# Two transfers, 120 rows and 8 rows, for the store of every 17th tile of a cross network kernel

## What is computed

```python
B, D, L = (16384, 4096, 6)
def step(x, wb):
    wi, bi = wb
    xw = jnp.matmul(x, wi)          # (B, 1)
    x_new = x0 * xw + bi + x
    return (x_new, None)
x, _ = jax.lax.scan(step, inputs, (w, b))   # x0 = inputs
```

## Time and profile before

| | us |
|---|---|
| median of 3 runs | 1284.51 (1283.15 to 1284.72) |
| the profiled execution | 1283.12 |
| its span, first to last instruction | 1281.4 |
| PE / PEld busy | 769.9 (60%) / 722.1 (56%) |
| DVE busy | 1149.6 (90%) |
| ACT / POOL busy | 99.0 (8%) / 5.1 (0%) |
| DMA | 537.69 MB, mean 420 GB/s |
| L275, finish of a tile | 126 of 4.464 |
| L262, transpose of 2048 columns | 252 of 2.288 |

### The profile page before, as it was taken

One profiled execution on the slowest core, in us unless ns is written; L12 is line 12 of the kernel. 1 busy time (PEld: TensorE's weight loads), 2 busy tenths in 40 slices (PEclk: granted clock), 3 DMA queues, 4 the chain that ended last, 5 costly groups with the idle time before them and its releaser, 6 DMA issues.

```text
span 1281.4 us, 19275 instructions
## 1 busy us (share of the span) xinstructions
PE 769.9 (60%) x8724; PEld 722.1 (56%) x8724; DVE 1149.6 (90%) x532; ACT 99.0 (8%) x326; POOL 5.1 (0%) x16
## 2 busy tenths in 40 slices
PE   5676666656566666556546655665655765665563
PEld 2665665555555565546546554565555654665453
DVE  5899998899988988989889898898898988989887
ACT  2000000000000000000000000000000000000000
POOL 1000000000000000000000000000000000000000
PEclk9878787777867867787787787777787678678776
DMA  9999999999999999999999999999999999999996
GB/s 353 402 425 430 429 433 427 428 431 432 430 430 432 429 432 431 430 420 427 425 421 422 415 427 421 422 425 423 422 425 421 422 427 422 420 426 424 425 420 281
DMA packets 38156, 537.69 MB, mean 420 GB/s; under 512 B 4296, under 2 KB 4488, under 8 KB 5632
## 3 DMA queue, kind: packets, MB, share of 16 engines
q1 hardware_dynamic: 18656, 268.64, 50.3%
q10 hardware_dynamic: 19488, 268.94, 49.4%
HBM read 269.12 MB, written 268.44 MB: 420 GB/s over the span
## 4 chain that ended last, share of the span: by engine, by line
DMA 77%; DVE 11%; PE 9%; ACT 2%; issue 1%; ACTq 0%; DVEq 0%
DMA out_dram<-tiles 62%; DMA tiles<-in_r_inputs_dram 14%; PE dots L333 9%; DVE tiles L275 6%; DVE blocks L262 4%; ACT spread L185 1%; DMA tiles<-in_L_rec_w_dram 1%; DVE tiles L297 1%; ACT weights L171 0%; PE turned L347 0%; PE scratch L311 0%; ACT c_last L176 0%; ACTq L162 0%; ACTq L165 0%; DVE tiles L223 0%
## 5 line engine op out<-in xcount | busy, mean ns | idle before, releaser
L333 PE MATMUL dots<-blocks,weights 128*64 128x128 f32 x8192 | 691.5, 348 | 401.5 <-DVE blocks L262 400.2
L333 PEld LDWEIGHTS dots<-blocks,weights 128*64 128x64 f32 x8192 | 656.6, 184 | 426.7 <-DVE blocks L262 425.3
L262 DVE STREAM_TRANSPOSE blocks<-tiles 128x2048 f32<-128x2048 f32 x252 | 567.1, 2288 | 107.1 <-issue 106.6
L275 DVE SCALAR_TENSOR_TENSOR tiles<-tiles,scale,c_last 128x4096 f32<-128x4096 f32 x126 | 562.5, 4464 | 0.0
L185 ACT ACTIVATE spread<-dots,group_mask 128x128 f32<-128x128 f32 x256 | 73.2, 369 | 1069.5 <-PE dots L333 1069.5
L347 PE MATMUL turned<-layer_sel,spread 128*128 128x8 f32 x512 | 67.9, 259 | 79.7 <-ACT spread L185 79.7
L347 PEld LDWEIGHTS turned<-layer_sel,spread 128*128 128x128 f32 x512 | 62.0, 191 | 95.1 <-ACT spread L185 95.1
L192 ACT ACTIVATE growth<-turned,ones 128x16 f32<-128x16 f32 x64 | 17.5, 274 | 80.3 <-PE turned L347 57.5
L269 DVE TENSOR_TENSOR_SCAN scale<-growth,cw 128x6 f32<-128x6 f32 x128 | 13.0, 141 | 4.9 <-ACT growth L192 4.9
L311 PE MATMUL scratch<-tiles,ones 6*128 6x512 f32 x16 | 8.9, 1134 | 13.4 <-ACT c_last L176 7.3
L311 PEld LDWEIGHTS scratch<-tiles,ones 6*128 6x128 f32 x16 | 2.5, 306 | 18.2 <-ACT c_last L176 8.8
(11 more groups left out here) (20 smaller groups left out, 7.2 us busy)
## 6 DMA issues: line engine op xcount, KB each, us to landing
tiles<-in_r_inputs_dram SPq DMA_DIRECT2D x128, 2048.0 KB, 13.7
out_dram<-tiles ACTq DMA_DIRECT2D x126, 2048.0 KB, 26.7
out_dram<-tiles ACTq DMA_DIRECT2D x8, 512.0 KB, 4.9
tiles<-in_L_rec_w_dram ACTq DMA_DIRECT2D x4, 96.0 KB
tiles<-in_L_rec_b_dram ACTq DMA_DIRECT2D x4, 24.0 KB
strips_b<-in_L_rec_b_dram SPq DMA_DIRECT2D x1, 96.0 KB, 11.3
strips_w<-in_L_rec_w_dram SPq DMA_DIRECT2D x1, 96.0 KB, 12.3
```

The costliest lines, as they stand in the source:

```text
L262: nc.vector.transpose(blocks[:, c, :, :].rearrange("p t n -> p (t n)"), tiles[:, at:at + TB, c * CH:(c + 1) * CH]).then_inc(blocks_ready, 1)
L275: nc.vector.scalar_tensor_tensor(out=tiles[:, s, :], in0=tiles[:, s, :], scalar=scale[:, batch % 2, t, L - 1:L], in1=c_last[:], op0=ALU.mu ...
L333: last = nc.tensor.matmul(dots[at:at + KM * Q, :, :, :], weights[:, c * KB + k:c * KB + k + KM, :], blocks[:, c, :, k * Q:(k + KM) * Q], s ...
```

## The change

`in_two(n)` holds for n = 9, 26, 43, 60, 77, 94 and 111 of the 128 tiles. `store` issues two transfers for these on ACT: rows 0 to 119, then rows 120 to 127, each adding 16 to the slot's semaphore. `stored_by(n)` is what the semaphore of tile n's slot stands at when tile n and all before it in that slot have been stored; SP and the end of ACT's program wait for it, in place of 16 for each store. Tiles 126 and 127, in four pieces each, are as before.

```diff
--- before.py
+++ after.py
@@ -19,6 +19,8 @@
 HALF_BANKS = 4
 S = 16
 PIECES = 4
+PART = 120
+EVERY, FIRST = 17, 9
 
 
 def cross_network(nc, x, w, b, out):
@@ -119,6 +121,12 @@
             turned_rows = w_turned[rows, :].rearrange("p (k q) -> p k q", q=Q)
             return into, turned_rows[:, :, 0:L * G].rearrange("p k (l j) -> p j l k", j=G)
 
+        def in_two(n):
+            return n % EVERY == FIRST
+
+        def stored_by(n):
+            return sum(32 if in_two(m) else 16 for m in range(n % n_slots, n + 1, n_slots))
+
         @block.sync
         def _(sp):
             for s in range(n_slots):
@@ -131,7 +139,7 @@
                     sp.dma_start(strips_w[:], w_strips).then_inc(strips_w_landed, 16)
             for n in range(n_slots, n_tiles):
                 s = n % n_slots
-                sp.wait_ge(y_stored[s], n // n_slots * 16)
+                sp.wait_ge(y_stored[s], stored_by(n - n_slots))
                 sp.dma_start(tiles[:, s, :], x[n * P:(n + 1) * P, :]).then_inc(x_landed[s], 16)
 
         @block.gpsimd
@@ -194,7 +202,12 @@
 
             def store(n):
                 act.wait_ge(tiles_done, n + 1)
-                act.dma_start(out[n * P:(n + 1) * P, :], tiles[:, n % n_slots, :]).then_inc(y_stored[n % n_slots], 16)
+                s = n % n_slots
+                if in_two(n):
+                    act.dma_start(out[n * P:n * P + PART, :], tiles[0:PART, s, :]).then_inc(y_stored[s], 16)
+                    act.dma_start(out[n * P + PART:(n + 1) * P, :], tiles[PART:P, s, :]).then_inc(y_stored[s], 16)
+                else:
+                    act.dma_start(out[n * P:(n + 1) * P, :], tiles[:, s, :]).then_inc(y_stored[s], 16)
 
             spread_dots(0)
             make_growth(0)
@@ -212,7 +225,7 @@
                               tiles[:, s, at]).then_inc(y_stored[s], 16)
             for s in range(n_slots):
                 last_stores = 1 if s < n_slots - TB else PIECES
-                act.wait_ge(y_stored[s], 16 * (n_rounds - 1 + last_stores))
+                act.wait_ge(y_stored[s], stored_by(n_tiles - n_slots + s) + 16 * (last_stores - 1))
 
         @block.vector
         def _(dve):
```

## The result

| | median us | lowest to highest | runs |
|---|---|---|---|
| before | 1284.51 | 1283.15 to 1284.72 | 6 |
| after | 1305.58 | 1297.14 to 1311.55 | 6 |

The ratio is 1.0158, 95% interval 1.0136 to 1.0181. The kernel is 21 us slower where 4.3 were forecast: the sign is right, the size is not, and the time lies outside the range. Some runs of a kernel fall into a slower state and are left out of times and ratios; here that is one, of the four with 25 cuts. The profiled execution took 1297.14 us, the fastest of the six, in a span of 1295.4 us. So the trace holds 14 of the 21 us, and what it shows of a cut (a tile stored in two pieces) is the low side.

What follows compares the result with a forecast made beforehand. One slow DMA engine of sixteen was taken to bound the kernel. Its seven added rows, 7 x 0.620 = +4.3 us, with everything else hidden, on the 1284.5 us median gave 1288.8 us, range 1262 to 1292 us.

Steps and rivals of the forecast that it cites:

- What bounds the kernel: DMA transfers: one slow engine of sixteen sets the pace, 0.620 us a row against 0.608 for the others.
- How rows fall on engines: A transfer uses the largest count up to 16 dividing its rows: 120 rows on 15 engines, 8 on 8.
- Which engine is slow: DMA engines: the slow one lies in both the 8 and the 15, so it gets seven rows more; 0.52.
- The trail of packets: Single packets followed per engine: the slow one took rows of w, and most likely of b.
- The rival of the spared engine: The slow engine is the one the 120-row pieces leave out: 20.4 us less, 1264.1 us; chance 0.22.
- the one of unchanged rows: Rival: the slow engine is one whose rows stay the same: 1284.5 us, no change; chance 0.17.
- Issues, waits, closing packets: Seven more ACT issues, 2.4 us, hidden; SP's waits for 32 and small closing packets cost nothing visible.
- The split transfer's own rate: Stores of split tiles: 0.608 to 0.620 us a row as now; at worst 4.9 us a tile, 34 in all.
- The row term, 7 x 0.620: Seven added rows on the slow DMA engine, from the 8-row pieces: +4.3 us.
- The pace stops mattering once the last load is issued: End of the run: all seven split tiles lie in front of that load, so their added rows count.
- The 120-row pieces run badly: Rival at the seven split tiles: 7 x 4.9 = 34 us, 1319 us at worst, some 1300 at half; chance 0.09.

Runs made afterwards that it cites:

- the four with 25 cuts: Runs of the kernel that makes the change's cut at row 120 in every fifth tile, 25 tiles in place of 7: 1345.85 us, ratio 1.0505 to before.
- four late ones: The change's cut, 120 and 8 rows, at tiles 60, 75, 90 and 105 only, against the kernel before: 1294.63 us, ratio 1.0078.
- early cuts: The change's cut, 120 and 8 rows, at tiles 9, 13, 17 and 21 only, against the kernel before: 1303.13 us, ratio 1.0129.
- the eight small pieces: Against the kernel before, eight tiles stored as 112, k and 16 - k rows, k from 1 to 8, last two on own semaphores: 1298.36 us, one execution.

## Why the prediction was wrong, step by step

- **What bounds the kernel: right.** One engine sets the pace before and after (share 0.06 at the end), and all lost time is ahead of the last load, which starts 14.0 us later in the profiled run.
- **How rows fall on engines: right.** 49 more packets are 15 and 8 engines; small pieces start on the same first engines.
- **Which engine is slow: right.** The trail of packets had it in both pieces; it is the fifth. The rival of the spared engine, 0.22, is ruled out by that, and so is the one of unchanged rows, 0.17.
- **Issues, waits, closing packets: nearly right.** ACT's busy time is the same 99.0 us. But a second transfer on a saturated stream is not free: 0.9 us a cut in the cut by columns, of which 0.6 falls at the cuts.
- **"The split transfer's own rate": this step failed.** I took the lower end, nothing, "since the piece is nearest to the 128-row store". It is near in size and not in shape. Alone, eight 120-row stores take 1.32 times as long as whole ones, and a row of the 8-row piece 2.5 us. In the kernel a cut costs 3.0 us in place of 0.62, and 2.0 with no row moved (112 and 16 rows).
- **The row term, 7 x 0.620: too small.** Sparing the slow engine its part in the 8-row piece gives back 10 us by the medians, 1.5 a cut, and 1.0 a cut by the two profiled runs.
- **"The pace stops mattering once the last load is issued": right here, not in general.** The change's last load starts 14.0 us later and its span ends 14.0 us later. The cut by columns and the kernel with 120, 4 and 4 rows lose 3.7 and 9.8 us in the last tiles.

An estimate from the shapes alone: on the slow engine 8 rows x 0.62 x 0.32 = 1.6 us, and the added row 0.62 at its own rate to 2.5 at the crowded one, which is 2.2 to 4.1 us a cut. Measured: 3.0 with seven cuts, 2.6 with 25, 2.6 with four late ones. The sum in its place would have been 1300 to 1313 us. It is made after the result, and its first term is right in size at best: the slow engine's own eight rows aren't slowed at the late cuts; what is lost beside the added row is lost ahead of them.

The rival "The 120-row pieces run badly" named the right piece, the right sign (a drop of the rate at the cut tiles) and a span of some 1300 to 1319 us that holds the result. It had 0.09, with no row for it or against it, and the range ended at 1292 for that reason. Its sum is not what happened: it doubled the time of the slow engine's own eight rows, which land at their old pace, and it had no price for the 8-row piece. That its span holds the result is in part luck.

What is shown: the loss goes by the cut (7, 25 and 4 late cuts); two thirds of it come without any row moved (14.1 of 21 us); the shapes alone have the rates above; taking the slow engine out of the 8 rows gives half of it back. What is only argued: that the cause of the rates is ways shared by neighbouring partitions, how the loss of a cut divides between the slow engine's added row and what the others do to it, and that their arrangement is what slows it in the tile ahead. What is open: the drift after early cuts; the one large step with 112 and 16 rows; the wide spread of times, 14 us in the change against 1.6 before; why whole columns in two pieces cost 0.9 us; why one engine is slow.

## To carry to other kernels

Don't price a store or load by its rows alone. Against transfers of all 128 rows, those of 120, 112 or 64 took 1.3 to 2 times as long for the rows on an engine, and those of 8 neighbouring rows 4 times. If you must cut, cut by columns: that was 0.9 us a cut in place of 3.0. At the end of a run look at the last loads too, for their delay is not hidden. Before you shift rows to relieve a slow engine, find which it is (small transfers of 1 to 8 rows on semaphores of their own show it), and compare the 2% that it is slow by with what the odd shape costs.

## What was not expected of the hardware

- 120-row loads take 1.94 times as long as 128-row loads (78.2 us against 40.3), 120-row stores 1.32 times (52.1 against 39.4).
- 28 stores of four rows (64 KB) from partitions 124 to 127, 1.8 MB of 539.5, make the kernel 67.5 us longer, 9.6 for each tile behind which four of them go.
- One engine of sixteen needs 0.620 us a row where the others need 0.608, by the trace of before, and one is late by 10 to 17 us in the late tiles of before, of the change, of the eight small pieces and of the late cuts. That it is the fifth was read in one trace, the eight small pieces. With this 2% it sets the pace of a kernel bound by transfers.
- A change at seven tiles widens the spread of a kernel's times from 1.6 us to 14 us.
